# Five adjacency loads issued as partitions 0 to 119 and 120 to 127 in a sparse graph-attention kernel

## The reference

```
hn = relu(layernorm(x));  h = hn @ W                     # W 128 x 128
e[i,j] = leaky_relu(h[i] . a[:128] + h[j] . a[128:], slope 0.2)
e = where(adj > 0, e, -9e15);  out = x + softmax(e, axis=1) @ h
```

## Time and profile before

| | |
|---|---|
| time, median of 3 runs | 799.86 us (799.39 to 799.94) |
| the profiled execution's own time | 800.1 us |
| its span, first to last instruction | 798.3 us |
| busy share: PE, DVE, ACT, POOL | 63%, 75%, 66%, 64% |
| DMA engines, mean busy share in the slices from 2 to 36 of 40 | 9 tenths or more |
| moved | 299.33 MB, mean 375 GB/s |
| mean granted TensorE clock | 0.701 |

### The profile page before, as it was taken

One profiled execution on the slowest core, in us unless ns is written; L12 is line 12 of the kernel. 1 busy time (PEld: TensorE's weight loads), 2 busy tenths in 40 slices (PEclk: granted clock), 3 DMA queues, 4 the chain that ended last, 5 costly groups with the idle time before them and its releaser, 6 DMA issues.

```text
span 798.3 us, 8948 instructions
## 1 busy us (share of the span) xinstructions
PE 505.1 (63%) x1823; PEld 230.5 (29%) x1855; DVE 598.9 (75%) x3132; ACT 526.8 (66%) x372; POOL 509.7 (64%) x520
## 2 busy tenths in 40 slices
PE   3677566666666566857766667667756766666621
PEld 3562222222222123323222223222322322322321
DVE  7957568766776767787767887677786787999893
ACT  3869767676767676676766677767677676767400
POOL 4653777656666665577766655655667776577672
PEclk9989758667667776585566766765577677586655
DMA  8999999999999999999999999999999999999510
GB/s 330 425 392 396 405 404 409 407 409 411 405 408 410 405 409 412 403 395 401 397 394 392 390 407 398 393 394 399 387 403 400 395 392 389 391 405 362 210 49 16
DMA packets 41127, 299.33 MB, mean 375 GB/s; under 512 B 11014, under 2 KB 13985, under 8 KB 24688
## 3 DMA queue, kind: packets, MB, share of 16 engines
q1 hardware_dynamic: 23264, 276.83, 85.9%
q0 software_dynamic: 15264, 17.60, 6.9%
q10 hardware_dynamic: 2544, 4.33, 1.5%
HBM read 304.18 MB, written 8.65 MB: 392 GB/s over the span
## 4 chain that ended last, share of the span: by engine, by line
DMA 53%; DVE 15%; issue 12%; ACT 9%; POOL 6%; PE 4%; POOLq 0%; ACTq 0%; DVEq 0%
DMA adj_buf<-in_adj 51%; ACT mask_buf L487 8%; POOL gathered L380 5%; DVE x_all L876 4%; PE banks L1108 2%; DVE stats L592 2%; DMA gathered<-table,index 1%; PE banks L1071 1%; POOL w_gathered L405 1%; DVE mv_all L596 1%; DVE rest L670 1%; DVE work L926 1%; DVE words L672 1%; DMA x_all<-in_x 1%; DVE words L668 0%
## 5 line engine op out<-in xcount | busy, mean ns | idle before, releaser
L487 ACT ACTIVATE mask_buf<-adj_buf,minus_half 128x2048 bf16<-128x2048 int32 x251 | 488.5, 1994 | 203.2 <-DMA adj_buf<-in_adj 202.7
L380 POOL DMA_INDIRECT gathered<-table,index x446 | 446.2, 1000 | 240.4 <-issue 144.8
L1108 PE MATMUL banks<-mask_buf,bit_ident 128*128 128x512 bf16 x992 | 378.3, 526 | 113.6 <-ACT mask_buf L487 110.3
L1108 PEld LDWEIGHTS banks<-mask_buf,bit_ident 128*128 128x128 bf16 x1024 | 107.7, 124 | 329.9 <-ACT mask_buf L487 192.6
L876 DVE SCALAR_TENSOR_TENSOR x_all<-gathered,weight,x_all 128x128 f32<-128x128 f32 x508 | 156.3, 348 | 7.0
L668 DVE MAX8 words<-banks 128x8 f32<-128x512 f32 x64 | 44.7, 698 | 124.0 <-PE banks L1108 123.9
L1104 PE MATMUL banks<-key_rows,ones_b 3*128 3x512 bf16 x64 | 32.2, 503 | 118.7 <-ACT mask_buf L487 118.2
L1149 PE MATMUL banks<-x_all,one_hot 128*128 128x128 f32 x128 | 43.7, 443 | 9.0 <-DVE x_all L876 9.0
L1104 PEld LDWEIGHTS banks<-key_rows,ones_b 3*128 3x128 bf16 x64 | 6.1, 95 | 140.3 <-ACT mask_buf L487 138.8
L672 DVE MAX8 words<-rest 128x8 f32<-128x512 f32 x64 | 44.5, 695 | 2.2
L670 DVE MATCH_REPLACE8 rest<-words,banks 128x512 f32<-128x512 f32 x64 | 43.5, 680 | 0.0
(11 more groups left out here) (169 smaller groups left out, 537.6 us busy)
## 6 DMA issues: line engine op xcount, KB each, us to landing
adj_buf<-in_adj SPq DMA_DIRECT2D x127, 2048.0 KB, 18.7
gathered<-table,index POOLq DMA_INDIRECT x446, 6.4
table<-gathered ACTq DMA_DIRECT2D x4, 1040.0 KB, 14.6
x_all<-in_x SPq DMA_DIRECT2D x3, 1024.0 KB, 10.9
out<-x_all SPq DMA_DIRECT2D x2, 1280.0 KB, 6.8
x_all<-in_x SPq DMA_DIRECT2D x2, 512.0 KB, 5.1
adj_buf<-in_adj SPq DMA_DIRECT2D x1, 1024.0 KB, 17.8
adj_buf<-in_adj SPq DMA_DIRECT2D x2, 512.0 KB, 17.1
```

The lines of the kernel that those rows point to most:

```text
L380: nc.gpsimd.indirect_dma_start(g_cols[buf][:, k, :], None, table, bass.IndirectOffsetOnAxis(index[:, buf, k:k + 1], 0), bounds_check=N, oo ...
L487: nc.scalar.activation(mask_buf[:, u], adj_buf[:, u], ACT.Sign, bias=minus_half[:]).then_inc(mask_ready, 1)
L1108: ins = mm(bank, bit_ident[:, h * PART_BITS + c], mask_buf[:, u, c * BIT_COLS:(c + 1) * BIT_COLS], start=False, stop=(h == PARTS - 1 and c ...
```

## The change

Five of the 127 big loads, the ones into units 2 and 3 of batches 4, 10, 16, 22 and 28, are issued as two transfers. The first carries partitions 0 to 119, the second partitions 120 to 127. The second has a semaphore of its own, `rest_loaded`, and ACT's `mask` waits for it too at these places.

```diff
+IN_TWO = ((4, 2), (10, 2), (16, 2), (22, 2), (28, 2))
+MOST = P - 8
@@
+        rest_loaded = sem("rest_loaded")
@@ load_two(i, u)
-                sp.dma_start(adj_buf[:, u:u + 2, :].rearrange("p u n -> p (u n)"), source).then_inc(adj_loaded[u // 2], 16)
+                place = adj_buf[:, u:u + 2, :].rearrange("p u n -> p (u n)")
+                if (i, u) in IN_TWO:
+                    sp.dma_start(place[0:MOST], source[0:MOST]).then_inc(adj_loaded[u // 2], 16)
+                    sp.dma_start(place[MOST:P], source[MOST:P]).then_inc(rest_loaded, 16)
+                else:
+                    sp.dma_start(place, source).then_inc(adj_loaded[u // 2], 16)
@@ mask(i, u)
                 act.wait_ge(adj_loaded[u // 2], 16 * (i + 1))
+                if (i, u // 2 * 2) in IN_TWO:
+                    act.wait_ge(rest_loaded, 16 * (IN_TWO.index((i, u // 2 * 2)) + 1))
```

## The result

The changed kernel takes 868.42 us (866.68 to 871.07, 4 runs) against 799.81 us, a ratio of 1.086 with an interval of 1.084 to 1.088. It is 68.6 us slower, 13.7 us for each of the five split loads. I had forecast 785 us, with 0.10 for any slowdown.

The account below looks back on a forecast made before the run. The prediction took transfers to bound the kernel, one late DMA engine setting the pace. Sparing it was to gain 12.5 us up to POOL's run plus 2.5 us of DVE's wait, 15 us: 785 us, own range 780 to 791.

Parts of the forecast that it names:

- one engine sets the pace: Loads of the kernel before: one late DMA engine, 3.6% slower than the others, sets the pace of all 127.
- the lower bound of the reserve: Up to 580: the fifteen other engines, at least 9 us ahead, have at least 9 - 2.6 = 6.4 us.
- unneeded estimate from 3.2% of busy time: Cause of lateness: instruction fetches, 3.2% if on one engine, against a laggard 3.6% slower; not needed for the sum.
- the sixteenth: Engine that had partitions 120 to 127, assumed to be the laggard and to rest during each large piece.
- the rival on the other side: Laggard is one of the eight engines getting small pieces, one row more at five loads: 803.2 us, chance 0.10.
- The price of a row: In the loads, a 16 KB row costs the laggard 5.675 x 0.93 / 8 = 0.66 us.
- a saving of 4 x 8 x 0.66 = 21.1 us: Laggard's relief up to the fourth split load: eight rows spared at each, 21.1 us.
- their whole reserve: What the other engines have gained by 580: 88 loads x 0.197 = 17.3 us, 14.7 after small pieces.
- The bounds of the range: The forecast's own range, 780 to 791: gain of 9 us above; 17 us and some 3 below.
- Its sum of nothing: By the skill's rule against two transfers to disjoint partitions, the change gains nothing and the time is 799.9 us.
- What was added costs nothing: Five more issues of 0.33 us hidden by SP's waits; ACT's added wait at worst one row, 0.66 us, already counted.
- The way to the end of the kernel: From 580: POOL's 65 transfers start earlier by the 12.5 us gained, then DVE's last 2.5 us wait goes too.

Follow-up runs that it names:

- three and four extra rows: Kernel before the change, plus in each of batches 2 to 23 a copy of three or four 16 KB rows within device memory: 798.92 and 814.03 us.
- stream: Loads-only kernel, 120 loads of 128 partitions, four in flight, four split into 120 and 8 partitions: whole loads 4.89 us apart, a split costs 8.2 to 8.9 us.
- stream_busy: The loads-only kernel with four split loads, plus 9000 one-column DVE memsets so that instructions must be fetched: loads 6.03 us apart instead of 4.89.
- shapes: Loads-only kernel, four loads of each shape, each after the one before has landed: 128 partitions 7.20 us, 0 to 119 11.63 us.
- halves: The changed kernel with its five loads split at partition 64 instead of 120: 859.08 us, 1.073.
- columns: The changed kernel with its five loads split by columns (3840 and 256), each piece over all 128 partitions: 800.0 us against 800.43, 1.0001.

## Why the prediction was wrong

**That one engine sets the pace: right.** The earlier trace rows read as one late engine, and the step between three and four extra rows bears it out: three engines took as much work for nothing, and the fourth took the kernel's time with it. One reading was a little off: until 739.4 a second engine still had packets, so one of the fifteen was only 747.20 - 739.4 = 7.8 us ahead and not 9, which puts the lower bound of the reserve at 5.2 us.

**What makes it late: right in kind, open in size.** The forecast had instruction fetches as an unneeded estimate from 3.2% of busy time. In `stream`, without fetches, the loads' queue keeps all 16 engines busy (100.6%) and loads are 4.89 us apart; in `stream_busy` it is 91.3% and 6.03 us, so the others have idle time. The trace of the kernel before shows the link itself. After 739.4 the packets of the loads come one at a time, from the one engine that is left, and the fetch at 739.98 stands between two of them. The queues from 739.95 to 741.64:

```profile
q1 hardware_dynamic: 2, 0.02, 4.6%
q14 instruction: 1, 0.01, 1.2%
```

The row behind the fetch takes 4.6% of 16 x 1.69 us, 1.2 us, and the 16 KB rows ahead of the fetch take 0.61 to 0.67. So the late engine is one that fetches instructions. That no other engine does isn't shown, nor whether fetches are all of its lateness; the gathers' part wasn't tried. A fetch costs far more than its packet: 1.0 us where 43 of them show 0.4% of 16 engines, which is 0.34 us each.

**Which engine: wrong.** The sum assumed the sixteenth. It is the fourth, one of the eight that get the small piece. I had this as the rival on the other side, with 0.10 and 803 us. Its sign was right, but its 3.3 us were a twentieth of the loss, and its cause, one more row on the late engine, wasn't what the loss came from. The Trainium skill's remark in "DMA: Bandwidth & Descriptors", "Latency and other measured facts", on engines 7 and 15 led me to the assumption; in this kernel it is neither, if the lowest-numbered engines take the extra rows.

**The price of a row: the step that failed.** "120 partitions lie on fifteen engines, eight rows each" held, by the 35 packets. But every term after it put a row at 0.66 us, whoever writes where. In the large piece it is 1.16 us by itself. The forecast costed the large piece as a saving of 4 x 8 x 0.66 = 21.1 us on one engine and at nothing on the fifteen; it costs 11.7 us a load, 58 us. The small piece was put at 0.66 us a load and cost 2.0. This step alone undoes the forecast, wherever the late engine sits: by `shapes` the fifteen have 4.4 us more work at each large piece, 4 x 4.4 = 17.6 us by the fourth, an estimate, and their whole reserve was put at 17.3. The bounds of the range came from the pace of the same shape of load and had no row for another shape, so they were no bounds. `halves` shows how little the reasoning about engines had to do with it.

**A rule was weighed, and the wrong one.** I set the Trainium skill's rule against two transfers to disjoint partitions ("DMA: Bandwidth & Descriptors", "Rules for kernel authors") aside as one about equal engines. It speaks of two halves, and two halves lost 58.3 us in `halves`. Its sum of nothing was nearer than mine, and even it has no price for what happened. The rule that bears on it, the port swizzle, I did not use.

**What was added costs nothing: right**, by `columns`.

**The way to the end of the kernel** (POOL's run from 580, DVE behind it) was never tested, since no time was gained up to there. What was lost went through: the two gaps at batch 4 are 6.5 + 6.6 = 13.1 us, and the launch lost 13.7 a split.

## What to carry to other kernels

A load that is cut by partitions is not the same load with fewer rows: measure the piece by itself, start to start, before any sum about who is relieved. Cut by columns, all partitions in each piece, a second transfer was free here (800.0 us against 800.43).

Where one DMA engine is late, a slow load cost more than elsewhere (about 14 us against 8 to 9), probably because it is still busy with older loads when the others get to the slow one. Extra copies of 1 to 8 rows find the late engine in a few runs.

## What the runs showed that I had not expected

- 64 partitions of 16 KB rows take 7.42 us, 128 take 7.20.
- One 8 KB instruction fetch every 5.3 us (43 in 230 us) turns a load every 4.89 us into one every 6.03 us, though the fetches are 0.4% of the DMA engines' time. The stretch 60 to 290 of `stream_busy` (us, busy by engine, clock, DMA share, GB/s):

```profile
60.00:290.00 230.00, 156.30 (x5510) 0.00 (x0) 1.00 0.92 354
```

- A split load delays the whole load ahead of it by as much as itself (+6.5 and +6.6 us).
